# Router casts off VectorE, raw weight pieces ahead in the DMA queue, and new places in a sixteen-step schedule

## The chip, the cores and the metric

One core of a Trainium2 chip. The time is the device time of one execution in microseconds; of the kernel before there are three runs, and their median is the number that counts.

## What is computed

One transformer-like layer on 4 sequences of 1024 tokens with 256 channels, all in float32. First a Mamba block, cut from the reference:

```python
xp, res = jnp.split(x @ W_in.T, 2, axis=-1)
xc = silu(conv1d(xp, conv_w, taps=4) + conv_b)
ssm = xc @ W_x.T                      # 16 of B, 16 of C, 1 of dt
dt = softplus(dt @ W_dt.T + b_dt)
h = exp(A * dt) * h + dt * B * xt     # per token, 512 channels x 16 states
y = einsum(h, C) + D * xt
x = layernorm(x + silu(y + res) @ W_out.T)
```

Then a mixture of 8 experts: a router softmax picks the top 2, each expert is 256 to 1024 (exact gelu) to 256, the two are weighted and added, and a second layernorm follows.

## The kernel before

The 4096 tokens are cut into 8 blocks of 512 (BLOCKS, T), two to a sequence; the states are 16 (STATE). `mamba` (L137) runs the blocks as iterations of sixteen **steps**, one for each state, and each step has four **quarters**, one for each group of 128 channels. In a quarter (n, q) of block i

- TensorE first turns the scaled input of state n into PSUM (`drive`, L458, matmul at L465, into one of two halves of `d_ps`; it waits until the scan two quarters before has read that half), then adds one or two quarters of products of an earlier state into `y_ps` (`sum_states`, L470, L478), then does what a table puts between;
- VectorE runs one scan over 512 tokens (`scan`, L1010, L1021), then what its table puts between;
- ScalarE works two steps ahead (LEAD): `scale` (L747, L756) makes the scaled input and `decays` (L764, L774) the decay, both from rings of three;
- GpSimd multiplies the scan's result with the row of C (`times_c`, L1317, L1327), in two halves a step. For blocks with an even number it also copies the last column away (L1322);
- SP's DMA queue loads the row of C for two steps on (`load_c`, L355) when GpSimd has finished the step before.

Four blocks are in work at a time. While block i is scanned, block i+1 (`front`, f) gets its silu, ssm projection, dt (z spread at L529, sizes at L543, L1056), its inputs dt*x (`inputs`, L1065, L1071) and their turned copies (`turn_u` on TensorE, L551, L557, read by `ut_out` on ScalarE, L868, L873); block i+2 (`early`) its input projection (`in_projection`, L496, L506, read by `xp_out`, L793) and convolution (`tap`, L1025); block i-1 (`back`) its gate, output projection (`out_projection`, L570, L577), residual and first layernorm; block i-2 (`place`) is routed. The gate products (`gate`, L485) and `skip` (L491) go straight into the sum of block i. The place of every such piece is written out by hand as a quarter (tables at L445 to L451 and the `at ==` lines), and each engine does its own in program order, so that a piece that has to wait holds up all behind it. Small results share six PSUM banks of 2 KB a partition (`BANK_OF`, L97); `bank_counts` (L123) derives the semaphore counts from the order of the names.

The router: `logits` (L594) on TensorE, `router_pick` (L1098) on VectorE: copy, top 8 of 8, their indices, three casts (L1117 to L1119) and a comparison with 0..7 that makes a one-hot (L1121); `router_member` (L1390) and `router_shift` on GpSimd; `ranks` (L607, L612, L615), which counts earlier tokens of each expert; `router_rank`, `router_sum`, `router_invert` and `router_place` (L1145) on VectorE, the last with a reduction (L1149) and the cast of the positions to integers (L1151). Then GpSimd sends 8 indirect DMAs of 128 rows each (`send_rows`, L1342, L1349). In the one-hot's place `router_spread` (GpSimd, L1414) puts the positions.

Beside this, the weights of four experts are cut into 64 **pieces** of 128 x 256, of which each is split into a rounded part and its rest: SP loads the raw piece, ScalarE makes the rounded part (`high_part`, L777, L779), GpSimd the rest (`low_part`, L1331, L1334), and SP stores both (`hand_on`, L366) and, right behind it, loads the raw piece that comes next. Eight of them go into each block, at PIECE_STEPS (L296); the ring is two (PARTS_RING).

After block 7, `end` of each engine finishes the last sum, projection and routing, and a table of slots is made. `experts` (L1506) then runs 71 slots of 128 rows, and `combine` (L1839) adds the two outputs and normalises.

## Time and profile before

| | us |
|---|---|
| median of 3 runs | 1548.41 (1547.02 to 1553.11) |
| profiled execution | 1544.33 |
| its span, first to last instruction | 1542.7 |
| TensorE busy (share of the span) | 1340.7 (87%) |
| VectorE | 1153.1 (75%) |
| GpSimd | 1036.7 (67%) |
| ScalarE | 1013.4 (66%) |

In the rows PE is TensorE, DVE VectorE, ACT ScalarE, POOL GpSimd and SP the engine whose queue loads and stores; SPq is that queue. L1021 is line 1021 of the kernel. A row of the timeline gives the start, the length, and in brackets how long the engine sat idle before it and who released it; x4 means four instructions merged into one row. Lengths of instructions that follow one another overlap: the pitch between them is shorter than the mean length. A row of a stretch gives start:end and its length, the busy us (and the count of instructions) of PE, PEld (TensorE's weight loads), DVE, ACT and POOL, then the granted TensorE clock as a share of full speed, the share of time that the DMA engines were busy, and GB/s. A row of a group of instructions ends with its busy us and the mean ns of one, then the idle time before them.

### The profile page before, as it was taken

How to read it: one execution, taken by the hardware profiler on the slowest of the kernel's cores; microseconds unless marked ns; L12 is line 12 of the kernel's file. 1: busy time of each engine (PE TensorE's matmuls, PEld its weight loads, DVE VectorE, ACT ScalarE, POOL GpSimd, SP SyncE). 2: the span in 40 equal slices, each digit the busy share in tenths (PEclk: the TensorE clock that was granted, in tenths of full speed). 3: DMA queues.
4: the chain of work that ended last, by engine and by line, in shares of the span. 5: the costliest groups of instructions: out<-in, count | busy, mean ns of one | idle time of the engine just before them, and what ended most of it. 6: DMA issues, size and time to landing. Idle time of an engine off the chain costs nothing. (4 is left out here: it accounts for less than half of the span.)

```text
span 1542.7 us, 29244 instructions
## 1 busy us (share of the span) xinstructions
PE 1340.7 (87%) x8828; PEld 1119.7 (73%) x8829; DVE 1153.1 (75%) x2010; ACT 1013.4 (66%) x1370; POOL 1036.7 (67%) x981
## 2 busy tenths in 40 slices
PE   4698898998998898998898898199999999999960
PEld 1377677777677677677677687189999999999860
DVE  5678888888988888988877887656666666666546
ACT  4898998979978978978987883234334334433324
POOL 3478787779878878878988998635444444444336
PEclk8699999999999999999999998599999999999985
DMA  7012223222322222322321326421453612311027
GB/s 262 21 56 86 72 65 102 69 87 73 91 86 75 91 84 75 104 70 76 103 73 59 110 76 225 138 74 53 149 167 110 217 41 85 119 38 42 25 70 275
DMA packets 85568, 150.12 MB, mean 97 GB/s; under 512 B 11042, under 2 KB 34210, under 8 KB 85476
## 3 DMA queue, kind: packets, MB, share of 16 engines
q1 hardware_dynamic: 70228, 116.39, 23.6%
q0 software_dynamic: 9888, 27.29, 5.3%
q10 hardware_dynamic: 5360, 5.26, 1.0%
q8 instruction: 52, 0.85, 0.2%
q14 instruction: 40, 0.33, 0.1%
HBM read 104.45 MB, written 44.45 MB: 97 GB/s over the span
## 5 line engine op out<-in xcount | busy, mean ns | idle before, releaser
L1327 POOL TENSOR_TENSOR arena<-arena 128x1024 f32<-128x1024 f32 x256 | 604.1, 2370 | 32.0 <-DVE arena L1021 17.0
L465 PE MATMUL d_ps<-ident,arena 128*128 128x128 f32 x2048 | 331.2, 287 | 59.3 <-DVE arena L1021 56.7
L465 PEld LDWEIGHTS d_ps<-ident,arena 128*128 128x128 f32 x2048 | 248.6, 147 | 177.5 <-issue 89.5
L1021 DVE TENSOR_TENSOR_SCAN arena<-arena,carry,d_ps 128x512 f32<-128x512 f32 x256 | 316.5, 1268 | 49.9 <-PE d_ps L465 47.1
L1021 DVE TENSOR_TENSOR_SCAN arena<-arena,d_ps 128x512 f32<-128x512 f32 x256 | 301.9, 1208 | 63.8 <-PE d_ps L465 61.1
L756 ACT ACTIVATE arena<-u_tok,b_tok 128x512 f32<-128x512 f32 x508 | 324.7, 714 | 5.6 <-PE d_ps L465 4.0
L478 PE MATMUL y_ps<-ident,arena 128*128 128x128 f32 x2048 | 301.8, 278 | 7.3 <-POOL arena L1327 7.3
L1663 ACT ACTIVATE h_t<-ht_ps 128x512 f32<-128x512 f32 x142 | 84.4, 595 | 295.9 <-PE ht_ps L1718 295.9
L774 ACT ACTIVATE arena<-dt,neg_a 128x2048 f32<-128x2048 f32 x128 | 255.5, 1996 | 2.1 <-DVE neg_a L1255 1.1
L478 PEld LDWEIGHTS y_ps<-ident,arena 128*128 128x128 f32 x2048 | 244.0, 144 | 8.5 <-POOL arena L1327 8.2
L1728 PEld LDWEIGHTS y_ps<-arena,h_parts 128*128 128x128 f32 x1704 | 214.6, 193 | 9.0 <-issue 4.2
L1703 PE MATMUL h_ps<-arena,xg_t 128*128 x852 | 216.7, 404 | 3.6 <-DVE xg_t L1798 2.9
L1728 PE MATMUL y_ps<-arena,h_parts 128*128 x1704 | 217.9, 284 | 1.8 <-DVE h_parts L1806 1.8
L1806 DVE TENSOR_TENSOR h_parts<-h_t,h_parts 128x512 fp32r<-128x512 f32 x142 | 98.3, 692 | 118.9 <-ACT h_parts L1665 117.5
L1703 PEld LDWEIGHTS h_ps<-arena,xg_t 128*128 128x128 f32 x852 | 157.5, 192 | 36.0 <-issue 5.7
L1608 POOL TENSOR_TENSOR rest<-b,tags 128x256 f32<-128x256 f32 x71 | 43.2, 609 | 138.0 <-DVE tags L1780 138.0
L1622 POOL DMA_INDIRECT expert_out<-y,dest x71 | 86.7, 1221 | 42.0 <-issue 23.6
L1598 POOL DMA_DIRECT2D xg<-expert_rows x71 | 41.4, 582 | 93.1 <-issue 90.6
L1792 DVE TENSOR_TENSOR h<-h_ps,b 128x512 f32<-128x512 f32 x142 | 91.7, 686 | 9.7 <-PE h_ps L1703 7.9
L1334 POOL TENSOR_TENSOR arena<-arena 128x256 fp32r<-128x256 f32 x64 | 46.8, 731 | 68.9 <-ACT arena L779 68.6
L1665 ACT CAST h_parts<-h_t 128x512 fp32r<-128x512 f32 x142 | 88.1, 620 | 4.5
L1813 DVE SCALAR_TENSOR_TENSOR y<-y_ps,tags,rest 128x256 f32<-128x256 f32 x71 | 34.4, 484 | 55.0 <-PE y_ps L1728 53.3
(220 smaller groups left out, 1712.4 us busy)
## 6 DMA issues: line engine op xcount, KB each, us to landing
arena<-c_rows SPq DMA_DIRECT2D x128, 256.0 KB
arena<-weight_parts SPq DMA_DIRECT2D x20, 1024.0 KB, 5.3
weight_parts<-arena SPq DMA_DIRECT2D x64, 256.0 KB, 3.7
xg<-expert_rows POOLq DMA_DIRECT2D x71, 130.0 KB
arena<-in_pieces SPq DMA_DIRECT2D x16, 512.0 KB, 8.7
arena<-in_pieces SPq DMA_DIRECT2D x64, 128.0 KB, 3.5
arena<-expert_out SPq DMA_DIRECT2D x16, 512.0 KB, 9.8
weight_parts<-arena SPq DMA_DIRECT2D x4, 1024.0 KB, 5.0
```

The source lines that it names most:

```text
L465: last = nc.tensor.matmul(d_ps[:, c % 2, j * P:(j + 1) * P], ub[:, g % U_RING, j, c * P:(c + 1) * P], t.ident[:], start=True, stop=True, i ...
L478: last = nc.tensor.matmul(y_ps[:, j, c * P:(c + 1) * P], h[:, g % H_RING, c, j * P:(j + 1) * P], t.ident[:], start=(n == 0 and c == 0), st ...
L756: nc.scalar.activation(ub[:, g % U_RING, j, :], u_tok[:, j, :], ACT.Identity, scale=b_tok[:, b % 2, j, n:n + 1]).then_inc(scaled, 1)
L774: nc.scalar.activation(decay[:, g % D_RING], dt[:, b % 2], ACT.Exp, scale=t.neg_a[:, n:n + 1])\
L1021: nc.vector.tensor_tensor_scan(h[:, g % H_RING, c, :], decay[:, g % D_RING, c, :], d_ps[:, c % 2, :], 0.0 if i % 2 == 0 else carry[:, n, c ...
L1327: nc.gpsimd.tensor_tensor(h[:, g % H_RING, lo:hi, :], h[:, g % H_RING, lo:hi, :], c_row[:, g % C_RING:g % C_RING + 1, :].broadcast_to([P, ...
L1622: pool.indirect_dma_start(out=d.y, out_offset=bass.IndirectOffsetOnAxis(ap=dest[:, k:k + 1], axis=0), in_=y[:, k, :], in_offset=None).then ...
L1665: nc.scalar.copy(h_parts[:, 0, lo:hi, :], h_t[:, lo:hi, :]).then_inc(h_high, 1)
L1703: last = nc.tensor.matmul(h_ps[:, g, :].rearrange("p (q n) -> p q n", n=PW), xg_t[:, k % 2, xp, c, :], w_r[:, bass.ds(e % W_RING, 1), q:q ...
L1728: last = nc.tensor.matmul(y_ps2[:, k % 2, 0:DIM], h_parts[:, hp, j, :], w_r[:, bass.ds(e % W_RING, 1), PIECES // 2 + j, wp, :].squeeze(1), ...
L1792: nc.vector.tensor_tensor(h[:, g * HALF:(g + 1) * HALF], h_ps[:, g, :], b1[:, bass.ds(e, 1), g * HALF:(g + 1) * HALF].squeeze(1), ALU.add) ...
L1806: nc.vector.tensor_tensor(h_parts[:, 1, lo:hi, :], h_t[:, lo:hi, :], h_parts[:, 0, lo:hi, :].bitcast(F32), ALU.subtract).then_inc(h_low, 1)
```

## The change

- Three casts of `router_pick` become reductions over an axis of length one. The one-hot's comparison reads 0..7 from the logits' PSUM bank, where one more matmul (identity times the row 0..7) puts them; the bank is freed by the comparison, and no longer by the copy of the logits.
- The cast of the positions moves from `router_place` on VectorE to the beginning of `send_rows` on GpSimd.
- On SP's queue the raw piece is loaded two steps after the piece that had its buffer, ahead of that step's store, and no longer behind the store one step after; PIECE_STEPS change.
- Nearly all tables change. TensorE: `turn(1)` from (2,0) to (1,3); logits from (4,1), (4,2), (5,0), (5,2) to (3,0), (3,3), (3,3), (4,0); ranks from (8,0) to (7,3); `turn_y` to (2,1), (2,1), (2,2), (2,2); ssm projection from (2,3), (3,0), (3,2), (3,3) to (2,3), (3,1), (3,1), (3,2); z spread from (4,2) to (5,0); sizes from (8,3), (9,1), (9,1), (9,2) to (8,3), (8,3), (9,3), (10,1); `turn_u` from (13,1), (13,2), (13,3), (14,0) to (13,0), (13,3), (14,0), (14,1); skip from (5,1), (12,3), (13,1), (14,2) to (4,3), (11,3), (11,3), (12,0).
- VectorE: add_sizes to (8,3), (8,3), (9,3), (10,3); inputs from (10,1), (11,1) to (9,3), (11,3); variance from (11,0) to (11,2); `router_rank` from (8,2) to (7,3), `router_sum` from (7,2) to (10,1), `router_place` from (15,2) to (15,1).
- ScalarE: the order within steps changes. `xp_out(2)` goes from step 0 back to step 15; `y_silu` from the end of step 1 to the start of 2; `turned_out` from 2 and 3 to 1 and 2; `ssm_out` from the start of 3 to its end; all four z parts between scale and decays of step 5; `size_exp` and `btok_out` to the end of 5; `router_exp` from 7 to 6; `normed` behind the scale of step 12; `xp_out(0)` and `(1)` to the ends of 11 and 12; `ut_out(0)` from the start of 14 to the end of 13.
- GpSimd: `router_member` and `router_shift` from the end of step 5 into step 6, behind the second product of step 5; `router_spread` from 12 to 7, `router_den` from 9 to 13, `rstds` from the end of 10 to 11, halo sums from 7 to 11; two sends in step 15 instead of one, and the other six at 1, 2, 2, 2, 4, 4 of the next iteration instead of seven at 0, 0, 1, 1, 3, 3, 4.

```diff
-BANK_OF = {"turn0": 0, "turn1": 1, "ssm": 0, "logits": 0, "z": 1, "z2": 2, "btok": 0, "out0": 0, "ranks": 1,
-           "zc0": 1, "zc1": 1, "zc2": 0, "zc3": 1, "out1": 0, "in0": 0, "in1": 1, "ut0": 0, "ut1": 0, "ut2": 0,
+BANK_OF = {"turn0": 0, "turn1": 1, "ssm": 1, "logits": 0, "z": 1, "z2": 2, "btok": 0, "out0": 0, "ranks": 1,
+           "zc0": 1, "zc1": 0, "zc2": 0, "out1": 0, "zc3": 1, "in0": 0, "in1": 1, "ut0": 0, "ut1": 0, "ut2": 0,
...
-        PIECE_STEPS = (1, 3, 5, 7, 9, 11, 13, 15)
+        PIECE_STEPS = (2, 4, 6, 7, 9, 10, 12, 14)
...
                     .then_inc(parts_stored[k % PARTS_RING], 16)
-                nxt = k - 1 + PARTS_RING
-                if k >= 1 and nxt < PARTED:
-                    sp.wait_ge(parts_stored[nxt % PARTS_RING], 16 * (nxt // PARTS_RING))
+
+            def fetch(k):
+                if k < PARTED:
+                    sp.wait_ge(parts_stored[k % PARTS_RING], 16 * (k // PARTS_RING))
                     hold(sp, held_sp)
-                    sp.dma_start(parts[:, nxt % PARTS_RING, 1], raw_piece(nxt))\
-                        .then_inc(raw_loaded[nxt % PARTS_RING], 16)
+                    sp.dma_start(parts[:, k % PARTS_RING, 1], raw_piece(k)).then_inc(raw_loaded[k % PARTS_RING], 16)
...
                         load_c(g + LEAD)
+                    piece = piece_of(*divmod(g - 2, STATE))
+                    if piece is not None:
+                        fetch(piece + PARTS_RING)
                     piece = piece_of(*divmod(g - 1, STATE))
                     if piece is not None:
                         hand_on(piece)
-                    if n == 4 and back:
+                    if n == 5 and back:
...
-                    if n == 7 and early and scans:
+                    if n == 9 and early and scans:
...
-        SUM_AT = [6 + k + max(0, 10 - k // 6) for k in range(4 * STATE)]
-        OUT_AT = (((7, 0), (7, 1), (7, 3), (7, 3), (7, 3), (8, 2), (8, 2), (8, 3)),
-                  ((10, 1), (10, 2), (10, 2), (10, 3), (10, 3), (11, 0), (11, 0), (11, 0)))
-        GATE_AT = ((4, 3), (6, 0), (6, 0), (6, 1), (7, 1), (7, 1), (8, 3), (9, 3))
-        IN_AT = (((11, 1), (11, 2)), ((12, 1), (12, 1)), ((15, 0), (15, 2)), ((15, 3), (15, 3)))
-        TAP_AT = (((11, 3), (12, 0), (12, 1)), ((13, 0), (14, 0), (15, 0)), ((15, 3), (16, 1), (16, 3)),
+        SUM_AT = [5 + k + max(0, 11 - k // 7) for k in range(4 * STATE)]
+        OUT_AT = (((7, 0), (7, 1), (7, 2), (7, 3), (7, 3), (8, 1), (8, 3), (8, 3)),
+                  ((10, 0), (10, 1), (10, 1), (10, 3), (11, 0), (11, 0), (11, 0), (11, 0)))
+        GATE_AT = ((6, 0), (6, 1), (6, 1), (6, 1), (7, 0), (7, 2), (9, 0), (9, 1))
+        IN_AT = (((11, 2), (11, 2)), ((11, 3), (12, 1)), ((15, 0), (15, 0)), ((15, 2), (15, 3)))
+        TAP_AT = (((11, 3), (12, 0), (12, 2)), ((13, 3), (14, 2), (15, 0)), ((16, 0), (16, 1), (16, 2)),
                   ((17, 0), (17, 1), (17, 2)))
...
                     if j == TT - 1:
+                        last = nc.tensor.matmul(bank("logits", p)[:, TT * EXPERTS:(TT + 1) * EXPERTS], t.ident[:],
+                                                t.iota_ef[:], start=True, stop=True)
                         last.then_inc(m_filled[bank_of("logits", p)], 1)
...
                     nc.vector.tensor_copy(logit[:].rearrange("p j e -> p (j e)"),
-                                          bank("logits", p)[:, 0:TT * EXPERTS])\
-                        .then_inc(m_freed[bank_of("logits", p)], 1)
-                    wait_freed(dve, "logits", p)
+                                          bank("logits", p)[:, 0:TT * EXPERTS]).then_inc(picked, 1)
+                    dve.wait_ge(picked, 4 * p + 1)
...
-                    nc.vector.tensor_copy(rows_of(p)[:, :, DIM + 1], idx[:, :, 0])
-                    nc.vector.tensor_copy(rows_of(p)[:, :, DIM + 3], t.token2[:, p, :])
-                    nc.vector.tensor_copy(ek[:], idx[:, :, 0:TOPK]).then_inc(picked, 1)
                     dve.wait_ge(picked, 4 * p + 3)
+                    nc.vector.tensor_reduce(rows_of(p)[:, :, DIM + 1], idx[:, :, 0:1], AXX, ALU.add)
+                    nc.vector.tensor_reduce(rows_of(p)[:, :, DIM + 3], t.token2[:, p, :].unsqueeze(2), AXX, ALU.add)
+                    nc.vector.tensor_reduce(ek[:], idx[:, :, 0:TOPK].unsqueeze(3), AXX, ALU.add).then_inc(picked, 1)
+                    dve.wait_ge(picked, 4 * p + 4)
                     nc.vector.tensor_tensor(
                         onehot[:].rearrange("p j k e -> p (j k) e"),
-                        t.iota_ef[:].unsqueeze(1).broadcast_to([P, TT * TOPK, EXPERTS]),
+                        bank("logits", p)[:, TT * EXPERTS:(TT + 1) * EXPERTS].unsqueeze(1)
+                        .broadcast_to([P, TT * TOPK, EXPERTS]),
                         ek[:].rearrange("p j k -> p (j k)").unsqueeze(2).broadcast_to([P, TT * TOPK, EXPERTS]),
-                        ALU.is_equal).then_inc(picked, 1)
+                        ALU.is_equal).then_inc(m_freed[bank_of("logits", p)], 1)
...
                 def router_place(p=p):
                     dve.wait_ge(spread, p + 1)
-                    if p == BLOCKS - 1:
-                        dve.wait_ge(rows_sent[p % 2], 16 * TT * TOPK * (p // 2))
+                    dve.wait_ge(place_chain, p)
                     nc.vector.tensor_reduce(rk[:], onehot[:], AXX, ALU.add).then_inc(pos_done, 1)
-                    dve.wait_ge(pos_done, 2 * p + 1)
-                    nc.vector.tensor_copy(pos[:, p % 2], rk[:]).then_inc(pos_done, 1)
-                    dve.wait_ge(pos_done, 2 * p + 2)
...
             def send_rows(b, m):
                 if m == 0:
-                    pool.wait_ge(pos_done, 2 * b + 2)
+                    pool.wait_ge(pos_done, b + 1)
+                    if b == BLOCKS - 1:
+                        pool.wait_ge(rows_sent[b % 2], 16 * TT * TOPK * (b // 2))
+                    nc.gpsimd.tensor_copy(pos[:, b % 2], rk[:]).then_inc(place_chain, 1)
+                    pool.wait_ge(place_chain, b + 1)
...
                 def router_member(p=p):
-                    pool.wait_ge(picked, 4 * p + 4)
+                    wait_freed(pool, "logits", p)
```

## Rows read from the trace of the kernel before

**Rows 1.** Blocks 2 and 7 as stretches: length, busy us of PE, PEld, DVE, ACT, POOL, clock, DMA.
```profile
...
273.60:385.60 112.00, 103.39 (x698) 82.91 (x697) 96.14 (x115) 98.34 (x122) 89.29 (x84) 0.97 0.24 76
...
841.30:943.20 101.90, 89.16 (x678) 78.31 (x678) 90.07 (x99) 75.04 (x93) 94.37 (x64) 0.98 0.28 87
```

**Rows 2.** The same columns, block 4 cut into groups of steps.
```profile
...
524.55:536.74 12.19, 12.19 (x101) 10.88 (x100) 9.46 (x8) 12.19 (x17) 9.86 (x10) 1.00 0.13 47
536.74:545.38 8.64, 7.43 (x48) 5.25 (x47) 8.28 (x23) 8.52 (x12) 7.39 (x6) 1.00 0.55 184
545.38:568.99 23.61, 23.61 (x146) 17.61 (x145) 18.44 (x24) 20.71 (x22) 22.65 (x25) 1.00 0.14 41
568.99:585.56 16.57, 14.92 (x105) 12.64 (x104) 14.96 (x19) 10.84 (x16) 10.05 (x12) 1.00 0.42 128
...
591.49:602.11 10.62, 7.58 (x54) 7.34 (x53) 5.42 (x5) 6.81 (x10) 10.30 (x11) 0.84 0.31 86
...
sum 114.18, PE 103.39 PEld 82.55 DVE 95.68 ACT 97.74 POOL 97.05; mean PE 12.92 PEld 10.32 DVE 11.96 ACT 12.22 POOL 12.13
```

**Rows 3.** Timeline of block 4, steps 6 and 7 (start, length, engine, line).
```profile
...
542.02 5.66 DVE L1021 TENSOR_TENSOR_SCAN arena<-arena,d_ps 128x512 f32<-128x512 f32 x5
...
546.22 0.25 POOL L1392 TENSOR_TENSOR member<-onehot 128x32 f32<-128x32 f32 x1
...
546.88 2.37 POOL L1327 TENSOR_TENSOR arena<-arena 128x1024 f32<-128x1024 f32 x1
...
```

**Rows 4.** Waits, 275 to 840 us (who <- for whom: total, times, longest).
```profile
DVE arena L1021 <- PE d_ps L465: 69.9, 79, 4.6
...
ACT arena L779 <- DMA arena<-in_pieces: 44.8, 15, 9.1
...
```

**Rows 5.** Timeline of block 2, steps 7 and 8, TensorE.
```profile
...
319.12 1.88 PE L486 MATMUL y_ps<-w_in,x_t 128*128 128x512 f32 x4
...
323.02 1.46 PE L577 MATMUL m_ps<-w_out,tmp 128*128 128x256 f32 x6
...
325.33 1.04 PE L615 MATMUL m_ps<-member,ones 128*128 128x32 f32 x8
...
```

**Rows 6.** Groups of VectorE's instructions, 275 to 840 us (busy us, mean ns).
```profile
...
L1117 DVE CAST xrow<-idx 128x4 f32<-128x4 uint32 x5 | 5.4, 1081 | 0.2
L1121 DVE TENSOR_TENSOR onehot<-iota_ef,ek 128x64 f32<-128x64 f32 x5 | 5.4, 1079 | 0.2
L1151 DVE CAST pos<-rk 128x8 uint32<-128x8 f32 x5 | 4.5, 908 | 0.2
...
L1149 DVE TENSOR_REDUCE rk<-onehot 128x8 f32<-128x64 f32 x5 | 1.0, 193 | 0.0
...
```

**Rows 7.** Timeline of block 7's end.
```profile
...
937.39 4.47 DVE L1151 CAST pos<-rk 128x8 uint32<-128x8 f32 x1
...
942.72 1.09 POOL L1349 DMA_INDIRECT expert_rows<-xrow,pos  x1 [0.89 <-DVE pos L1151]
...
```

**Rows 8.** Timeline of block 3, step 13.
```profile
...
476.68 0.36 SPq L375 DMA_DIRECT2D arena<-in_pieces  x1
...
478.68 1.99 ACT L774 ACTIVATE arena<-dt,neg_a 128x2048 f32<-128x2048 f32 x1
...
482.06 0.41 ACT L779 CAST arena<-arena 128x256 fp32r<-128x256 f32 x1 [1.39 <-DMA arena<-in_pieces]
...
483.00 1.11 PE L557 MATMUL m_ps<-ident,y_u 128*128 128x128 f32 x4 [3.43 <-ACT u_tok L873]
...
485.01 1.28 DVE L1021 TENSOR_TENSOR_SCAN arena<-arena,carry,d_ps 128x512 f32<-128x512 f32 x1 [4.55 <-PE d_ps L465]
```

**Rows 9.** DMA issues on the page (count, KB each, us to landing).
```profile
...
weight_parts<-arena SPq DMA_DIRECT2D x64, 256.0 KB, 3.7
...
```

**Rows 10.** Timeline of block 4, VectorE's inputs.
```profile
...
571.24 1.20 DVE L1071 TENSOR_TENSOR y_u<-dt,xc 128x1024 f32<-128x1024 f32 x1
...
579.87 2.30 DVE L1071 TENSOR_TENSOR y_u<-dt,xc 128x1024 f32<-128x1024 f32 x1
...
```

More of the change, by code:

```diff
@@ L953, in step @@
                     if place and n == 2:
-                        turned_out(0)
-                    if front and n == 3:
-                        ssm_out()
-                    if place and n == 3:
                         turned_out(1)
-                    if front and n == 5:
-                        z_part(2)
-                    if front and n == 6:
-                        btok_out()
-                    if place and n == 7:
-                        router_exp()
-                    if early and n == 12:
-                        xp_out(e, 0)
-                    if back and n == 12:
-                        normed()
-                    if early and n == 13:
-                        xp_out(e, 1)
                     if front and n == 14:
-                        ut_out(0)
                         ut_out(1)
@@ L977, in step @@
                         scale(g + LEAD)
-                    if front and n == 4:
+                    if place and n == 1:
+                        turned_out(0)
+                    if front and n == 5:
                         z_part(0)
                         z_part(1)
-                    if front and n == 6:
+                        z_part(2)
                         z_part(3)
+                    if back and n == 12:
+                        normed()
+                    if early and n == 15:
+                        xp_out(e, 2)
                     if 0 <= g + LEAD < STEPS:
@@ L986, in step @@
                         high_part(piece_of(i, n))
-                    if back and n == 1:
-                        y_silu()
                     if back and n == 2:
                         yt_copy()
-                    if front and n == 6:
+                    if front and n == 3:
+                        ssm_out()
+                    if front and n == 5:
+                        btok_out()
                         size_exp()
+                    if place and n == 6:
+                        router_exp()
                     if front and n == 7:
                         size_log()
+                    if early and n == 11:
+                        xp_out(e, 0)
+                    if early and n == 12:
+                        xp_out(e, 1)
+                    if front and n == 13:
+                        ut_out(0)
             iterations(act, step)
@@ L1433, in end @@
                     router_shift()
-                    for m in range(1, 4):
+                    for m in range(2, 4):
                         send_rows(BLOCKS - 3, m)
@@ L1481, in step @@
                         router_weigh()
-                    if place and n == 5:
-                        router_member()
-                        router_shift()
-                    if back and n == 10:
-                        rstds()
                     if place:
-                        for m, when in enumerate((15,)):
+                        for m, when in enumerate((15, 15)):
                             if n == when:
```

66 lines of the change are left out of this document (35 added, 31 removed).

## The prediction

> **What bounds the kernel now.** I read the busy time by stretches first. The span has a scan part (eight blocks of sixteen steps, 55 to 943 us), a short joint to about 1004 us, and the expert and combine parts, which the change doesn't touch. Block 2 begins at 273.6 and block 7 at 841.3 [rows 1], so a middle block takes 567.7 / 5 = 113.5 us; everything below is a sum over such blocks. In block 4 TensorE is busy 103.4 of 114.2 us, ScalarE 97.7, GpSimd 97.1 and VectorE 95.7 [rows 2]: no engine is full, and what sets the pace differs from step to step. The same rows, by steps, show it. In steps 4 to 5 and in steps 7 to 9 TensorE is busy for all of 12.19 and 23.61 us while VectorE has gaps; these are TensorE's. In step 6 VectorE is the fuller (8.28 of 8.64). In step 13 nobody is but GpSimd: 10.62 us for VectorE work of 5.42. VectorE's scans follow at 5.66 / 5 = 1.13 us [rows 3], so four of them alone are 4.5 to 4.7 us, the floor of a step.
>
> The waits of the five blocks say the same: the scan waits 69.9 us for its d_ps input from TensorE (79 times), which is 14 us a block; ScalarE waits 44.8 us for raw weight pieces [rows 4].
>
> **The change, part by part.** A tally of each step, as the larger of two sums: TensorE's (four drives and about four and a half state sums, at 4 x 0.11 us each by the pitch of L615, 3.5 to 4.0 us, plus what stands between) and VectorE's (4.6 plus its extras). From [rows 5]: a gate product is 2 of the 4 matmuls that take 1.88 us at 0.43 each, so 0.86; an output product 2 of six in 1.46, so 0.43; the ranks' ten about 1.1; logits of one tile 4 x 0.11 = 0.44; a skip 8 x 0.11 = 0.87. The other 512-wide products (ssm, sizes, input halves) are taken like a gate. For steps 7 to 9 of before this gives 7.8 + 8.1 + 7.4 = 23.3 against 23.61 measured, so I trust it to about 0.3 a step.
>
> 1. Casts off VectorE. The three casts of the pick and the cast of the positions work on 4 to 8 elements, yet the means are 1081 ns (L1117) and 908 ns (L1151), against 193 ns for the reduction L1149 beside them, which handles 64; the comparison L1121 also has 1079 [rows 6]. One L1151 took 4.47 us [rows 7]. The long ones end as GpSimd's product ends. They become reductions (0.16 to 0.19), the comparison reads its constants from PSUM, and the position cast moves to GpSimd. Over the five blocks the excess is 5 x (0.92 + 0.92 + 0.74) = 13 us of VectorE, 2.6 a block. Not all is on the path: a delayed pick lets TensorE finish its gates. By the tally step 6 after it is TensorE's: 4.0 + four gates 3.4 + 0.2 = 7.6, against 8.64. I take -1.0 for step 6, and nothing in 15, where TensorE's 3.96 + 3.44 = 7.4 covers it. GpSimd's cast of 8 elements has no row; between its member addition, 0.25 [rows 3], and a send, 1.09 [rows 7], I take 0.25 (nearest in size), beside other work. The matmul that puts the constants into PSUM is one of 0.11, twice that at most.
>
> 2. DMA queue. Before, SP issues a store and, behind it, the next raw piece, for use one step on. In block 3 it was issued at 476.68; ScalarE, free at 480.67, got it at 482.06, and only then made the copy that TensorE waited for: 3.43 us of TensorE, 4.55 of VectorE [rows 8]. After, the raw piece goes ahead of the store of its step and, where the spacing is 2, two steps early. No step of the queue is removed: per step one c row, at most one fetch, one store. The new wait, for the store of one step earlier, holds back the x loads behind it; a store of 256 KB lands in 3.7 us [rows 9] and a step is 7, so zero. I count 1.4 us a block here, inside step 13.
>
> 3. turn_u and ut_out. ut_out(0) moves from step 14 to the end of 13, and turn_u spreads from three quarters of 13 to (13,0), (13,3), (14,0), (14,1). The copy is then ready about when (13,3) asks, and the later ones one quarter apart. Step 13: tally 5.4, plus 1 to 2 of wait left, so 7.0 against 10.62: -3.6. This is the largest term, with bounds -1 (the wait only moves to step 14) and -5.2 (none left).
>
> 4. Steps 4 to 5: gate and two logits leave; what stays is one logit, a skip and the z spread: 5.0 + 5.1 = 10.1 against 12.19: -2.1. It needs ScalarE two microseconds earlier there; ssm_out, turned_out and two z parts move behind decays(6), which gives 2.1 us back, so it just fits. Bounds 0 and -2.6.
>
> 5. Steps 7 to 9: ranks moves into step 7 (4.0 + five outputs 2.15 + two gates 1.7 + ranks 1.1 = 8.9), which relieves 8 and 9 (7.3, 6.8): 23.0, -0.6.
>
> 6. Other steps: three taps instead of two in step 0 (+0.7), ssm and logits together in 3 (+0.3), step 2 -0.3; 10 to 11 6.6 + 10.2 against 16.57, +0.2; 12, 14, 15 even. Together +0.9. More work lands in one quarter (two skips at (11,3)); I put +0.5 a block on that.
>
> 7. A price that VectorE keeps: inputs (L1071) reads two SBUF tiles. In block 4 its first half took 1.20 us, the second 2.30 [rows 10]. The first half runs where GpSimd stands idle for ScalarE's piece; if item 2 ends that idleness, it can take the longer form. Between 0 and +1.1 a block, I take +0.8. The Trainium skill (page "SBUF — State Buffer", section "Who interferes with whom") states that a VectorE instruction with two SBUF inputs contends with a GpSimd one that reads SBUF; it speaks against the change here, and the two durations fit it. By it alone the term would be the +1.1, and the sum 2 us worse.
>
> Sum for block 4: -1.0 - 3.6 - 2.1 - 0.6 + 0.9 + 0.5 + 0.8 = -5.1, and -5.0 for the mean block. Five blocks -25. Block 1 has no router and no casts, but items 3 and 4: -3 (estimate). Block 0 has neither router nor output projection, and its turn_u wait has other neighbours: -2 (estimate). Block 7 has TensorE light and GpSimd at 94.4 of 101.9 [rows 1]: the long cast of 4.47 goes, but the first send of that block now stands on GpSimd with a second (1.1 us) and the position copy ahead of the last product: -1 and +0.5. Total -30.5. The profiled execution took 1544.33 us, so 1513.8; the median of the three runs is 4.1 higher, at 1548.41, and the forecast is given on its scale: **1518 us**.
>
> **The rivals.**
> *TensorE stays the bound.* Its stretches at 100% [rows 2] are only reshuffled; cast time was hidden and step 13's wait moves to 14. Then item 3 gives -1, item 4 -0.7, item 1 -0.5, and +1 of clumping: about -1.2 a block, -8 in all: 1540. For it: TensorE's work is the same plus one matmul. Against: it idles 10.8 us a block, most of it in 13 and 11.
> *More than forecast.* Every block comes down to TensorE's 103.4 busy: 5 x -10 and -4 at the ends: 1494.
> *Slower: the ranks wait.* router_member moved behind the second product of step 5 in GpSimd's order. In block 4 the member ran at 546.22 and that product from 546.88 to 549.25 [rows 3], 12.5 us after step 6 began (536.74). ranks is now wanted at (7,3), by the tally 7.6 + 6 = 13.6 after it. GpSimd's low part of the piece at step 2 now waits for ScalarE's silus, and three sends (1.1 each) follow it, so it may be later than today. Each microsecond past 1.1 is paid by TensorE, and by VectorE's rank behind it, in six blocks. At 5 us past, all of the gain is gone; at 7, with ScalarE's item 4 not fitting, the time is 1548 + 10 = 1558. For it: GpSimd lags VectorE most just there. Against: its shorter steps before and the c rows' distance leave it a microsecond.
> *It doesn't do what it says.* The reductions, or the PSUM comparison, are held by GpSimd like the casts: 13 us of VectorE and 4.3 in block 7 come back, a third on the path: 1525 to 1530. L1149 at 193 ns, always beside a long cast's place, speaks against [rows 6].
>
> **How the numbers follow.** Forecast (1506 to 1531) 0.60; TensorE stays the bound (1531 to 1548) 0.18, half of it within 0.5%; more than forecast 0.07; doesn't do what it says 0.04; ranks wait 0.11, of it 0.08 slower and 0.03 the same. A measurement tells about 0.5%, 7.7 us, from no change. Faster 0.60 + 0.09 + 0.07 + 0.04 = 0.80; same 0.12; slower 0.08. The range reaches down to items 3, 4 and 7 at their good bounds, 5 x -3 more, 1502, and up into the TensorE case: 1541. Left out: about 0.05 below, 0.14 above.
>
> **What would show it.** L1117, L1119 and L1121 near 0.2 us in every block; step 13 at 7 us, no wait of TensorE's L557 over 2 us; the piece wait of ScalarE under half of 44.8; steps 4 to 5 near 10; a middle block near 108.5. Wrong if a middle block keeps over 112; if VectorE's rank or TensorE's ranks matmuls wait over 2 us; if the first half of inputs stays at 1.20 my item 7 is wrong, in the good direction.

## The result, and the profile after

| | median us (runs) | ratio to before, 95% |
|---|---|---|
| before, beside it | 1549.59 (1547.02 to 1553.11) | |
| after | **1496.41** (1495.88 to 1496.80) | 0.9655 (0.9634 to 0.9676) |

The kernel is 53 us faster. The forecast was 1518 with a range down to 1502: the direction was right, the size too small by 22 us, and the time lies below the range. The page of the profiled execution (1495.88 us), its span and busy times:

```profile
span 1494.2 us, 29280 instructions
...
PE 1320.8 (88%) x8844; PEld 1100.9 (74%) x8845; DVE 1122.4 (75%) x2002; ACT 1011.9 (68%) x1370; POOL 1042.4 (70%) x989
```

Against the table of before, TensorE's and VectorE's busy time fell, by 20 and 31 us, though TensorE got one matmul more a block. The span fell by 48.5 us. By the starts of the blocks' first scans that is 1.5 before block 0, 5.1 in block 0, 4.1 in block 1, 35.3 in the five middle blocks (567.7 to 532.4) and 2.4 from block 7's start to the end. The other 4 to 5 us between 48.5 and 53 are scale: the profiled execution of before was the quickest of its runs.

Blocks 2 to 6 as stretches, with the columns of [rows 1], one block and the sum of the five:

```profile
262.80:368.80 106.00, 101.00 (x700) 79.93 (x699) 91.72 (x114) 98.11 (x122) 89.95 (x85) 1.00 0.27 81
...
sum 532.40, PE 503.50 PEld 400.22 DVE 465.58 ACT 488.44 POOL 471.88; mean PE 100.70 PEld 80.04 DVE 93.12 ACT 97.69 POOL 94.38
```

The sum of the same five blocks in the kernel before:

```profile
sum 567.70, PE 516.84 PEld 414.31 DVE 482.02 ACT 490.11 POOL 472.49; mean PE 103.37 PEld 82.86 DVE 96.40 ACT 98.02 POOL 94.50
```

VectorE runs the scans, so its time divides the gain: 482.0 - 465.6 = 16.4 us less work and 85.7 - 66.8 = 18.9 us less standing still. ScalarE and GpSimd work as much as before.

Block 4 by steps, cut as in [rows 2] (in order: steps 0 to 3, 4 to 5, 6, 7 to 9, 10 to 11, 12, 13, 14 to 15):

```profile
476.88:502.25 25.37, 21.97 (x146) 16.93 (x145) 22.48 (x22) 25.31 (x28) 22.23 (x20) 0.93 0.23 79
502.25:513.15 10.90, 10.67 (x88) 9.40 (x87) 9.24 (x8) 10.90 (x16) 10.43 (x9) 1.00 0.27 87
513.15:522.29 9.14, 7.74 (x46) 5.25 (x45) 6.19 (x23) 9.02 (x12) 8.49 (x9) 1.00 0.32 98
522.29:545.87 23.58, 23.58 (x153) 18.29 (x152) 18.94 (x22) 22.24 (x27) 22.96 (x21) 1.00 0.39 115
545.87:561.60 15.73, 15.73 (x105) 12.70 (x104) 13.39 (x21) 10.96 (x16) 12.34 (x14) 1.00 0.34 110
561.60:568.00 6.40, 6.30 (x52) 5.57 (x51) 5.88 (x6) 6.25 (x11) 6.24 (x5) 1.00 0.09 34
568.00:573.09 5.09, 5.07 (x45) 4.58 (x44) 5.09 (x7) 3.48 (x4) 4.93 (x6) 1.00 0.17 46
573.09:584.27 11.18, 11.18 (x80) 8.93 (x79) 10.60 (x14) 10.07 (x15) 10.55 (x15) 1.00 0.27 79
sum 107.39, PE 102.24 PEld 81.64 DVE 91.80 ACT 98.24 POOL 98.17; mean PE 12.78 PEld 10.21 DVE 11.47 ACT 12.28 POOL 12.27
```

Step 13 went from 10.62 to 5.09 and is now full of VectorE work. Step 6 did not get shorter (8.64 to 9.14), though VectorE's work in it fell from 8.28 to 6.19: something else sets it now. Waits of the five middle blocks, 262.8 to 795.2 us, columns as in [rows 4]:

```profile
DVE arena L1024 <- PE d_ps L468: 60.9, 86, 2.6
...
PE m_ps L528 <- DVE onehot L1123: 6.8, 5, 1.4
```

The scan's wait for TensorE fell from 69.9 to 60.9 us (the rows of before have the same values for its own five blocks), in more and shorter pieces: 86 with a longest of 2.6, where there were 79 with a longest of 4.6. ScalarE's 44.8 us for raw pieces are gone. New is TensorE's wait for the comparison, which now frees the PSUM bank. The groups that answer to [rows 6], 275 to 800 us (L1119 was the cast L1117, L1123 is the comparison):

```profile
L1119 DVE TENSOR_REDUCE xrow<-idx 128x4 f32<-128x4 uint32 x5 | 0.8, 161 | 0.2
...
L1123 DVE TENSOR_TENSOR onehot<-m_ps,ek 128x64 f32<-128x64 f32 x5 | 1.1, 224 | 0.2
```

The cast (1081 ns) became 161 ns and the comparison (1079) 224 ns. The position cast, now on GpSimd, is short there but for one of eight, at 922 us, when the blocks' scans are over (minimum, median, maximum in ns):

```profile
L1346 POOL CAST pos<-rk x8: 187/198/1208, 370.9 to 937.6; 128x8 uint32<-128x8 f32 x8
```

### The profile page after: what moved, and what is told of

Its sections match the earlier page's. It is cut to its first block and busy times, and to the rows that moved or that the text cites. A ratio compares the mean times of both kernels' runs of the same rounds, so it can differ in the third digit from the quotient of the medians.

```text
span 1494.2 us, 29280 instructions
## 1 busy us (share of the span) xinstructions
PE 1320.8 (88%) x8844; PEld 1100.9 (74%) x8845; DVE 1122.4 (75%) x2002; ACT 1011.9 (68%) x1370; POOL 1042.4 (70%) x989
## 5 line engine op out<-in xcount | busy, mean ns | idle before, releaser
L468 PEld LDWEIGHTS d_ps<-ident,arena 128*128 128x128 f32 x2048 | 240.5, 144 | 149.6 <-issue 70.8
L468 PE MATMUL d_ps<-ident,arena 128*128 128x128 f32 x2048 | 323.0, 282 | 30.8 <-DVE arena L1024 26.0
L1024 DVE TENSOR_TENSOR_SCAN arena<-arena,carry,d_ps 128x512 f32<-128x512 f32 x256 | 313.5, 1264 | 45.0 <-PE d_ps L468 44.8
L481 PE MATMUL y_ps<-ident,arena 128*128 128x128 f32 x2048 | 298.0, 274 | 12.3 <-POOL arena L1326 12.3
L481 PEld LDWEIGHTS y_ps<-ident,arena 128*128 128x128 f32 x2048 | 239.3, 142 | 14.1 <-POOL arena L1326 14.1
L1721 PE MATMUL ht_ps<-ident,h 128*128 128x128 f32 x568 | 73.8, 273 | 0.5 <-DVE h L1795 0.5
```

The costliest lines, as they stand in the source:

```text
L468: last = nc.tensor.matmul(d_ps[:, c % 2, j * P:(j + 1) * P], ub[:, g % U_RING, j, c * P:(c + 1) * P], t.ident[:], start=True, stop=True, i ...
L481: last = nc.tensor.matmul(y_ps[:, j, c * P:(c + 1) * P], h[:, g % H_RING, c, j * P:(j + 1) * P], t.ident[:], start=(n == 0 and c == 0), st ...
L1024: nc.vector.tensor_tensor_scan(h[:, g % H_RING, c, :], decay[:, g % D_RING, c, :], d_ps[:, c % 2, :], 0.0 if i % 2 == 0 else carry[:, n, c ...
```

## The experiments

Each time is the median of its runs. The ratio is to runs of the kernel before that stood beside them, in four sets with medians of 1551.7, 1549.15, 1549.21 and 1548.99 us. In the expectations A is the theory of the prediction; the other letters are rivals, each said where it first stands.

### One part alone, on the kernel before

`b_casts`: only the reductions, the PSUM constants and the position cast on GpSimd. `b_turnu`: only

```diff
-for j, when in enumerate(((13, 1), (13, 2), (13, 3), (14, 0))):
+for j, when in enumerate(((13, 0), (13, 3), (14, 0), (14, 1))):
```

with `ut_out(0)` at the end of ScalarE's step 13. `b_dma`: only the order on SP's queue, `hand_on` without its load and `fetch(piece + PARTS_RING)` ahead of it, with the old PIECE_STEPS. `b_all3`: the three together.

> The kernel before with the cast part alone (reductions, constants from PSUM, position cast on GpSimd). Theory A (the gain of 53 us is a sum of parts, none of them over half): the casts are worth some 8 to 12 us here, because step 6 falls from 8.4 only to about 7.6 (TensorE's products, and turn_b now waits for the comparison to free bank 0) and step 15 in two blocks by 1.1, block 7 gains its 4.5 us: 1538 to 1541. Theory B (the casts and what they hold up are most of the gain): 1520 or less. Theory C (step 13's wait is most of it): within 4 us of before, 1545 to 1549.

> The kernel before with the new places of turn_u and of ut_out(0) alone. Theory A: step 13 falls from 9.95 on average to about 7 (the late raw piece no longer stands ahead of ut_out(0), since with the old places of the pieces there is one at step 13, so it does stand there still): -12 to -18 us, 1531 to 1537. Theory B: -5 or less. Theory C: -25 or more.

> The kernel before with the new order of the DMA queue alone. ScalarE's wait for raw pieces should fall from 9 us a block to under 3. Theory A: only the part inside step 13 reaches the end, 1.4 to 2 us in the blocks where it stood (3, 4, 5), and some 0 to 1 elsewhere: -5 to -9 us, 1540 to 1544. Theory B: nothing, 1547 to 1549. Theory C (step 13's wait is most of the gain, and the DMA most of that wait): -15 or more.

> The three parts together on the kernel before, all other tables old. Theory A: their sum and a little more, since step 13 is freed only by two of them together (5.3 a block instead of 9.95): 1515 to 1522, and the other tables are worth the 20 to 25 us that remain. Theory B and C: 1505 or less, the other tables only reshuffle.

| | us | ratio, 95% | to before |
|---|---|---|---|
| b_casts | 1539.75 | 0.9926 (0.9907 to 0.9945) | -12 |
| b_turnu | 1541.82 | 0.9942 (0.9921 to 0.9963) | -10 |
| b_dma | 1512.43 | 0.9750 (0.9731 to 0.9769) | **-39** |
| b_all3 | 1507.45 | 0.9710 (0.9678 to 0.9742) | -44 |

`b_casts` came as expected, `b_turnu` gave less, `b_dma` far more, and `b_all3` lies between its two expectations. The queue's order alone is nearly three quarters of the whole gain; the prediction had given it 1.4 us a block. The parts add up to 61 and give 44 together, for two of them cure the same wait: step 13, 9.95 us on the mean of the five middle blocks, falls to 6.52 in `b_dma`, to 7.44 in `b_turnu`, and only to 5.40 in `b_all3` (steps are measured here from first scan to first scan). The other tables and the new PIECE_STEPS bring the rest, 0.9710 to 0.9655: some 8 us. PIECE_STEPS were not tried by themselves. `b_dma` in its five middle blocks, and its steps 10 to 11 and 13 of block 4:

```profile
552.91:567.79 14.88, 14.33 (x101) 12.05 (x100) 14.20 (x19) 10.38 (x16) 10.92 (x12) 1.00 0.43 134
...
573.72:580.39 6.67, 5.94 (x54) 5.67 (x53) 5.43 (x5) 5.18 (x8) 6.51 (x6) 1.00 0.31 90
...
sum 544.00, PE 507.18 PEld 403.79 DVE 479.67 ACT 491.37 POOL 471.97; mean PE 101.44 PEld 80.76 DVE 95.93 ACT 98.27 POOL 94.39
```

Step 13 falls from 10.62 to 6.67 without `turn_u` being touched. Of 567.7 - 544.0 = 23.7 us, VectorE's work is 2.4 and its standing still 21.3. By steps, on the mean of the five blocks, it is 3.4 us in step 13 and 1.5 in step 11, and little elsewhere. So the queue took away the waits, and what `after` has on top (11.6 us in these blocks) goes with less work: 14.1 us of VectorE's. The casts and the comparison are 15 us shorter, and the inputs are 2.4 longer again.

### What held the queue

The waits of the SP queue itself, 54 to 945 us, in the kernel before (the first row is the c rows' normal pace):

```profile
SPq L42 <- POOL arena L1327: 674.8, 113, 29.3
SPq L42 <- PE y_ps L486: 92.1, 6, 17.7
```

After:

```profile
SPq L42 <- PE y_ps L489: 2.8, 4, 1.4
```

SP waited six times, 92.1 / 6 = 15.4 us on the mean, for the gate products. That is the wait ahead of the x load (`sp.wait_ge(gates_done, i + 1)` at step 7), whose last gate stood at (9,3). The timeline of block 4, steps 7 to 10, of the kernel before shows what stood behind it:

```profile
554.50 0.32 SPq L363 DMA_DIRECT2D arena<-c_rows  x1
...
568.61 0.33 SPq L428 DMA_DIRECT2D x_t<-in_x_t  x1
...
569.52 0.37 SPq L369 DMA_DIRECT2D weight_parts<-arena  x1
570.00 0.37 SPq L375 DMA_DIRECT2D arena<-in_pieces  x1
...
574.72 0.41 ACT L779 CAST arena<-arena 128x256 fp32r<-128x256 f32 x1 [7.01 <-DMA arena<-in_pieces]
575.20 0.72 POOL L1334 TENSOR_TENSOR arena<-arena 128x256 fp32r<-128x256 f32 x1 [6.04 <-ACT arena L779]
```

For 14 us SP issues nothing. Then the x load, a c row, the store and only at 570.00 the raw piece of step 9 go out; ScalarE stands 7.01 us and GpSimd 6.04. ScalarE is late from here on, and when it comes to step 13 another piece holds it, as in [rows 8]. The new `fetch` loads the piece ahead of this wait; the whole change also moves the wait two steps on and the last gate to (9,1). `b_xload` and `b_swap` take these apart, on the kernel before:

```diff
-                    if n == 7 and early and scans:        # b_xload
+                    if n == 9 and early and scans:
```
```diff
+                nxt = k - 1 + PARTS_RING                  # b_swap: the load ahead of the store, same step
+                if k >= 1 and nxt < PARTED:
+                    ...
                 sp.wait_ge(low_done, k + 1)
```

> The kernel before with one digit changed: SP's load of the next x block stands at step 9 instead of step 7. There it waits for the last gate product (9,3), 15 to 18 us in each of six blocks (92.1 us in all), and the c row, the store and the next raw piece stand behind it. Theory D (the held queue is where the 38 us of the queue's order come from: ScalarE then waits 7 us for the piece of step 9, comes late to ut_out(0), and TensorE and VectorE wait in step 13): most of it comes back by this digit alone, -15 to -32 us, 1518 to 1535. Theory E (it is the place of the raw piece behind the store in the ring, at every step): -5 or less.

> The kernel before with the raw piece issued ahead of the wait for low_done and of the store, within the same step, for use one piece on; nothing else. Theory E (place behind the store): most of the 38 us, -20 to -35, 1516 to 1531. Theory D (the wait of step 7 ahead of it, or the lead): -3 to -10, since the piece of step 9 is still issued only when the gates are done.

`b_xload` took 1524.91 us, 0.9845 (0.9797 to 0.9892): **one digit gives -24**. `b_swap` took 1531.74, 0.9887 (0.9846 to 0.9929): -17. Both together (`b_xswap`), and the x load moved on top of the full queue order (`b_xdma`):

> The kernel before with both small edits: x load at step 9, and the raw piece ahead of the store within the step (one step of lead). Theory H (lateness of the raw piece at ScalarE is the whole cause, however it comes about): the wait for raw pieces falls under 10 us and the time to that of the queue's new order, 1510 to 1516. Rival (the two-step lead has a worth of its own): 1518 to 1524.

> The kernel before with the queue's new order and the x load at step 9. Theory H: the lead covered the held queue already, so nothing is added to the 1512.4 of the order alone: 1509 to 1514. Rival (the held queue costs something beside the raw pieces, by c rows that come late to GpSimd, 6 us of waits in the profile of the order alone): 1502 to 1508.

`b_swap` came between its two expectations. `b_xswap` took 1521.11, 0.9817 (0.9792 to 0.9841), -28, where the rival had its range: the two mend mostly the same thing, and both together are still some 10 us short of `b_dma`, whose raw piece is also fetched two steps ahead. Some 5 us of that are in step 13, with 7.59 us on the mean of the five blocks against 6.52. `b_xdma` took 1516.7, 0.9787 (0.9767 to 0.9807), -32: no gain on top of `b_dma`, and 4 us more in the medians, though the two intervals just touch. In the profiled executions it is 4.6 us, and 3.6 of them are steps 6 and 7 of one block, in which two of the pick's instructions were held and not one:

```profile
413.77 1.79 DVE L1120 CAST xrow<-idx 128x4 f32<-128x4 uint32 x1
...
415.73 2.35 DVE L1124 TENSOR_TENSOR onehot<-iota_ef,ek 128x64 f32<-128x64 f32 x1
```

ScalarE's wait for raw pieces, 54 to 945 us, goes with the times but for that last case. Of the 67.5 us of before, 42 stand ahead of the pieces of step 9, those behind the x load. Before, `b_xload`, `b_xswap`, `b_dma`, one fence each:

```profile
ACT arena L779 <- DMA arena<-in_pieces: 67.5, 25, 9.1
```
```profile
ACT arena L779 <- DMA arena<-in_pieces: 26.4, 21, 4.9
```
```profile
ACT arena L779 <- DMA arena<-in_pieces: 17.2, 16, 3.1
```
```profile
ACT arena L782 <- DMA arena<-in_pieces: 4.5, 1, 4.5
```

67.5, 26.4, 17.2, 4.5 us of waiting stand beside 1549, 1525, 1521, 1512 us (`b_swap` has 55.5 and 1532, with step 9's 40 still in it; `b_xdma` 4.1 and 1517). In `b_dma` the queue itself waits for the gates as long as ever:

```profile
SPq L42 <- PE y_ps L489: 92.7, 6, 17.3
SPq L42 <- DMA weight_parts<-arena: 23.2, 6, 4.0
```

So the long wait in the queue costs nothing by itself. What cost was the load that stood behind it and was needed soon. The second row is the new wait for the store, 23.2 us in six times. `b_xdma` has neither this wait nor most of the first (28.7 us left), and it is no faster.

### One part undone, from the kernel after

`a_dma`, `a_turnu` and `a_casts` are the reverse of the three parts above, but for one thing: `a_dma` has the old order with the new PIECE_STEPS. `a_x7` puts the x load back to step 7.

> The changed kernel with the old order of the DMA queue (raw piece behind the store, for use one piece on), new places of the pieces. Theory A: ScalarE waits again for raw pieces, up to 3 us each, but its lead of 8 to 14 us in steps 9 to 15 hides most; +2 to +8, 1498 to 1504. Theory C: step 13's wait comes back, +15 or more.

> The changed kernel with turn_u and ut_out(0) at their old places. There is no raw piece at step 13 any more, so TensorE waits for ScalarE's decay only, about 2.2 us as in block 1 of before. Theory A: +2.2 to 3 in seven blocks, +15 to +21: 1511 to 1517. Theory B: under +5. Theory C: +25 or more.

> The changed kernel (1496.4) with the casts put back on VectorE as before, all tables new. Theory A: +10 to +15 us (VectorE is nearer to the bound now, and each cast that meets a GpSimd product costs up to 2.4 us; the wait of turn_b for bank 0 goes, -1.5 a block): 1503 to 1511. Theory B: +30 or more. Theory C: +0 to +3.

> The changed kernel with the x load back at step 7. Its last gate is at (9,1), so SP is held 10 to 12 us a block again. Theory H (the lead covers it): +0 to +5, 1496 to 1501. Rival: +10 or more.

| | us | ratio to before, 95% | to after |
|---|---|---|---|
| a_dma | 1524.43 | 0.9840 (0.9799 to 0.9881) | **+28** |
| a_turnu | 1502.42 | 0.9707 (0.9668 to 0.9747) | +6 |
| a_casts | 1511.08 | 0.9764 (0.9725 to 0.9804) | +15 |
| a_x7 | 1496.36 | 0.9660 (0.9644 to 0.9677) | 0 |

`a_turnu` cost less than theory A had, `a_dma` far more; `a_casts` and `a_x7` came as expected. From this side the queue's order is again the largest term, but not by the same wait. In `a_dma` the x load stands at step 9, no wait of SP's for the gates is left, and still ScalarE waits 82 us for raw pieces. Of these, 35 are at the pieces of step 7 and 32 at those of step 10, in every block: each is the second of two pieces that PIECE_STEPS now puts one step apart, and by the old order it is loaded only behind the store in its own step. So this +28 is the price of the old order with the new places, and doesn't confirm the price of the held queue, which rests on `b_xload`. With only the x load back at step 7 SP waits 65 us for the gates and ScalarE 23.0 us for raw pieces, and the time stays; that ScalarE has the lead to bear it is the likely reason, not tested. `a_dma`, then `a_x7`:

```profile
ACT arena L781 <- DMA arena<-in_pieces: 82.0, 23, 5.8
```
```profile
ACT arena L784 <- DMA arena<-in_pieces: 23.0, 8, 5.4
```

Either place of the x load will do once the piece is fetched first. The single runs of `a_casts` differ as no other kernel's do: 1492.54 in the profiled one, 1510.67 to 1512.66 in the others. Its profile therefore shows an execution in which the casts cost nothing, and no row of it is used here; the +15 is that of the others. `a_sbuf`, next, was also quickest in its profiled execution, so its rows show less than its median.

### The comparison's operands

`a_sbuf`: the kernel after, with the comparison reading 0..7 from SBUF again.

```diff
-                        bank("logits", p)[:, TT * EXPERTS:(TT + 1) * EXPERTS].unsqueeze(1)
-                        .broadcast_to([P, TT * TOPK, EXPERTS]),
+                        t.iota_ef[:].unsqueeze(1).broadcast_to([P, TT * TOPK, EXPERTS]),
```

With it the copy of the logits frees the bank again, and the matmul of the constants is gone.

> The changed kernel with the comparison reading 0..7 from SBUF and the copy freeing the logits' bank, as before; the three reductions stay. TensorE's turn_b no longer waits 1.6 us a block for the bank (five of five blocks). Theory A (that new wait is on the path): TensorE reaches drive (6,2) earlier, -1.5 a block where the comparison isn't caught, but the comparison with two SBUF inputs is held by GpSimd up to 2.2 us in some blocks: -4 to +4, 1492 to 1500. Rival (the bank wait is hidden under the pick anyway): 0 to +8, by the held comparison alone.

It took 1518.24 us (1509.0 in the profiled run, up to 1522.1), 0.9816 (0.9774 to 0.9857): +22 for one instruction a block, where little was expected. The row of that instruction, eight blocks, in ns:

```profile
L1122 DVE TENSOR_TENSOR onehot<-iota_ef,ek x8: 225/1012/6991, 301.4 to 936.2; 128x64 f32<-128x64 f32 x8
```

The same comparison takes 224 ns from PSUM and up to 6991 from SBUF. It was 1079 ns on the mean in the kernel before, beside a cast of 1081. One by one, in blocks 3 and 4 of that kernel, it is the one or the other:

```profile
424.37 1.78 DVE L1117 CAST xrow<-idx 128x4 f32<-128x4 uint32 x1
...
426.32 0.22 DVE L1121 TENSOR_TENSOR onehot<-iota_ef,ek 128x64 f32<-128x64 f32 x1
...
539.36 0.17 DVE L1117 CAST xrow<-idx 128x4 f32<-128x4 uint32 x1
...
539.71 2.39 DVE L1121 TENSOR_TENSOR onehot<-iota_ef,ek 128x64 f32<-128x64 f32 x1
```

Of the seven picks up to 947 us, five have a long cast (1.47 to 2.75 us) and a short comparison, the other two a short cast and a long comparison (2.39 and 2.33). The long one ends within 0.1 us of the end of one of GpSimd's products. Mostly the first of the pick's instructions that meets a product is held and what follows gets through, but not always: in one block a second cast took 0.71 us, and in `b_xdma` a cast and the comparison were both held. So the casts had to go *and* the comparison had to leave SBUF. With the casts alone gone only the comparison is left to meet the product, and it can pay more: 1.63, 6.99, 0.23, 6.97 and 0.23 us in blocks 2 to 6 of `a_sbuf`. The 6.99 runs beside three products of GpSimd that follow one another without a gap (407.64 to 414.63), so it did not get in between them. Step 6 takes 14.1 us in those two blocks and 7.8 in the other three. `a_sbuf`'s 1518 us are no better than `a_casts` with both undone (1511). The Trainium skill (page "SBUF — State Buffer", section "Who interferes with whom") states that a VectorE operation with two SBUF inputs contends with a GpSimd one that reads SBUF, that a copy or cast in a 2-port mode does too, that whoever issues first has the shared pair of ports for the whole instruction, and that on trn2 a reduction never contends. This case agrees: 161 ns for the reduction against 1081 for the cast, 224 against up to 6991 for the comparison. That these casts ran in such a mode no row shows.

### What sets step 6 now

The timeline of block 3, step 6, of the kernel after:

```profile
407.37 0.22 DVE L1123 TENSOR_TENSOR onehot<-m_ps,ek 128x64 f32<-128x64 f32 x1
...
407.65 0.42 PE L528 MATMUL m_ps<-ident,ssm 16*128 16x16 f32 x4 [1.43 <-DVE onehot L1123]
...
408.00 2.84 PE L489 MATMUL y_ps<-w_in,x_t 128*128 128x512 f32 x6
...
410.68 0.60 PE L468 MATMUL d_ps<-ident,arena 128*128 128x128 f32 x4
...
411.32 2.45 DVE L1024 TENSOR_TENSOR_SCAN arena<-arena,carry,d_ps 128x512 f32<-128x512 f32 x2 [2.53 <-PE d_ps L468]
```

TensorE waits 1.43 us with a small turn (L528, `btok` in BANK_OF) for the bank that the comparison frees, runs three gates (six matmuls) at (6,1), and the scan then waits 2.53 for its input. Two causes are possible, the bank and the gates. `a_btok` takes the wait for the comparison away, by another bank for that turn; `a_btokg` also moves one gate a quarter on; `a_btokg2` spreads them where VectorE's pick covers them.

```diff
+EARLY_BANK = {"btok": 3, ...}                             # a_btok, with "btok": 1 in BANK_OF
-GATE_AT = ((6, 0), (6, 1), (6, 1), (6, 1), (7, 0), (7, 2), (9, 0), (9, 1))
+GATE_AT = ((6, 0), (6, 1), (6, 1), (6, 2), (7, 0), (7, 2), (9, 0), (9, 1))   # a_btokg
+GATE_AT = ((5, 3), (6, 0), (6, 1), (6, 1), (6, 2), (7, 2), (9, 0), (9, 1))   # a_btokg2
```

> The changed kernel with turn_b's output in bank 1 (bank 3 for block 0) instead of bank 0, which the comparison frees late. In the profile after, TensorE waits 1.6 us for it in each routed block, and the scan (6,2) 2.6 us. Theory F (that wait is on the path): step 6 falls from 9.2 to about 7.8, -6 to -9 us over six blocks: 1487 to 1491. Rival G (the three gates behind it set the step anyway): 0 to -3.

> As a_btok, and one gate moved from (6,1) to (6,2), behind the drive that the scan waits for. Theory F: a little better than a_btok, -1 more. Rival G: this is the part that counts, -4 to -6 against 1496.

> As a_btokg (1492.1), with the five gates of steps 6 and 7 one or two quarters earlier: (5,3), (6,0), (6,1), (6,1), (6,2) instead of (6,0), (6,1), (6,1), (6,2), (7,0). If the scan's waits in steps 6 and 7 are TensorE's gates in quarters where VectorE has nothing beside the scan, (7,1) loses its 1.1 us and (6,0) gets 0.5: -2 to -4, 1488 to 1490. Rival (the sum over steps 5 to 8 is TensorE's whatever the places): within 1 us.

`a_btok` 1496.13, 0.9664 (0.9623 to 0.9704): the wait for the comparison is gone and the time stays. That doesn't clear the bank, for the other bank is late too. Block 4:

```profile
516.18 0.42 PE L528 MATMUL m_ps<-ident,ssm 16*128 16x16 f32 x4 [0.59 <-ACTq L855]
```

TensorE now waits for ScalarE, which reads z out of that bank, and step 6 of this block falls from 9.14 to 8.41 us (from 9.21 to 8.65 on the mean of five). `a_sbuf` shows what is left: the copy frees the bank early, the turn of this block waits for nobody, the three gates stand at (6,1) as in `after`, and step 6 takes 7.8 us in the three blocks whose comparison took 1.63 us or less. So the late bank is on the path, at some 1.3 us a block, of which `a_btok` gets back 0.6.

`a_btokg` 1492.08, 0.9642 (0.9601 to 0.9684), -4 in the median, within its interval of nothing. `a_btokg2` **1489.80**, 0.9616 (0.9600 to 0.9632), all four runs between 1489.56 and 1490.40: below every run of the kernel after, and the lowest median of all versions. The largest part of its gain over `a_btok` is in step 7, 8.69 to 7.79 us on the mean of the five blocks, for the gate at (7,0) is gone from there; step 6 moved by 0.2. Places and bank both count, then, and a bank that is free in time together with the new places was not tried. The scan's wait for TensorE, 54 to 945 us, falls from 102.0 us in `after`, first below, to 89.8 in `a_btokg2`, second, in more pieces:

```profile
DVE arena L1024 <- PE d_ps L468: 102.0, 132, 4.9
```
```profile
DVE arena L1024 <- PE d_ps L468: 89.8, 142, 4.9
```

## Why the prediction was too small

**The step that failed** is item 2: "I count 1.4 us a block here, inside step 13". Alone it measured 23.7 / 5 = 4.7 us in a middle block and 39 us in all. The item read the queue at the one place where TensorE was seen waiting for a late piece, and counted that piece's own 1.39 us. It followed ScalarE's wait of 44.8 us [rows 4] no further, and never asked what SP was waiting for. The place, step 13, was right: the five middle blocks gave 4.7 us a block there against the 3.6 of item 3. The cause and the reach were not. The queue's order alone gives 3.4 us in step 13 and 1.5 in step 11, where the forecast had +0.2 for steps 10 to 11. The view for it, the waits of the SP queue, holds the answer in one row: 92.1 us for L486. "No step of the queue is removed" was true and misleading, for a wait of 15 us stood in the middle of it, ahead of a load that was due: with that wait moved and nothing else, `b_xload` gave 24 us. The diff had even moved that wait (step 7 to 9, and the last gate from (9,3) to (9,1)), and the forecast passed over both as moves.

Point by point:

- **Item 1, casts**: -1.0 in step 6 held for the casts alone: block 4's step 6 is 8.64 before and 7.62 in `b_casts`. In the whole change it rose by 0.5, since three gates now stand together at (6,1) and the turn ahead of them waits for the comparison to free the bank, a wait that the item left out. "Nothing in 15" was low: step 15 fell by 0.6 us on the mean in `b_casts`. In size the item was low. VectorE's work fell by 14.1 us over five blocks beyond `b_dma`, the pick's and the position's 15 less the inputs' 2.4, near the 13 forecast as excess; but the forecast put only 5 of it on the path, and undoing the item costs 15 us, doing it alone gives 12. The durations came as forecast (161 and 224 ns).
- **The new wait, "so zero"**: it is not zero in the queue (23.2 us in `b_dma`), but nothing shows that it costs anything, as said.
- **Item 3, turn_u**: "This is the largest term" was wrong. Step 13 did fall, by 5.5, past the bound of 5.2, but `b_dma` has 3.95 of it. The new places alone are worth 10 us from before and 6 from after, about one a block. The bounds had been set from what TensorE's wait could shrink to, with the wrong cause behind it.
- **Item 4, steps 4 to 5**: -1.3 against -2.1. **Item 5**: 0.0 against -0.6. **Item 6**: steps 0 to 3 of block 4 rose by 1.4 where +0.7 was taken; steps 10 to 11 fell by 0.8 where +0.2 was taken, and with the queue's order alone they fell by 1.7.
- **Steps 14 to 15**, taken as even, gave 1.4. The forecast had let TensorE's products cover step 15. That part of them runs over into the next block's steps 0 to 3, which rose by as much, is likely and not shown.
- **Item 7, inputs**: nearly nothing against the kernel before, and not as forecast. The first half takes 3.14 us in two of five blocks and 1.22 to 1.42 in the others, and the second half, which took up to 2.90 before, takes 1.20 in all five. Block 3 of the kernel after:

```profile
436.07 3.14 DVE L1074 TENSOR_TENSOR y_u<-dt,xc 128x1024 f32<-128x1024 f32 x1
...
451.35 1.20 DVE L1074 TENSOR_TENSOR y_u<-dt,xc 128x1024 f32<-128x1024 f32 x1
```

The ten of the five middle blocks take 15.8 us before, 16.1 after and 13.7 in `b_dma`. So the queue's order by itself made them shorter, and the new places took 2.4 us back, 0.5 a block.

- **Blocks 0, 1 and 7**: -5.1, -4.1, and -2.4 from block 7 on, against -2, -3 and -0.5. The queue's wait is in blocks 0 and 1 as well; `b_dma` gives 2.7 and 4.0 there.
- **The scale**: 4.1 us were added for the median over the profiled execution. After, the two agree within 0.6 us, so the whole addition was missed.

In us of the trace: forecast -30.5, measured -48.5, of which 10 in the middle blocks, 3.1 and 1.1 in blocks 0 and 1, 1.9 from block 7 on and 1.5 ahead of block 0.

Of the rivals, **more than forecast** (1494, given 0.07) is where it came out, though not by its mechanism: the middle block is at 106.5 and not at 103.4, and TensorE's own busy time fell to 100.7. The **ranks wait** did not come: VectorE's rank waits 1.0 us for TensorE's ranks over five blocks, and TensorE's ranks do not stand among the waits. **TensorE stays the bound** was wrong in its time and right in part: the scan's wait for it fell only from 69.9 to 60.9 us, and nearly half of it now lies in steps 6 to 8.

**Left open**: why the last 10 us between `b_xswap` and `b_dma` need two steps of lead, beyond their place in step 13; what the new PIECE_STEPS are worth by themselves; and why `a_casts` varies from run to run. Raw pieces can be fetched further ahead only with a ring of three, which was not tried.

## What to carry to other kernels

When an engine waits for a DMA, look at the issuing queue's own waits before pricing the transfer: a load that is due may stand behind a semaphore wait for something that is needed much later, and then its place in the queue can be worth more than its bytes. Put the load that is due first, and the one with slack, with its wait, behind it. And when small VectorE operations show durations far over their size, change together all neighbours that GpSimd can hold: mending one can hand the wait to the next. When an experiment removes a wait, look whether another has taken its place before calling the first one harmless.

## What the runs showed of the hardware

- A comparison of 64 elements a partition with both inputs in SBUF took 225 to 6991 ns; with one of them in PSUM, a mean of 224 ns.
- In seven picks of the kernel before either the cast of 4 elements was long, at up to 2.75 us, or the comparison behind it; in one block of `b_xdma` both were (1.79 and 2.35 us). A long one ended within 0.1 us of a GpSimd product's end, and one of 6.99 us lasted over three such products.
- Casts written as reductions over an axis of one take 150 to 161 ns for 4 to 8 elements, and a GpSimd cast of 8 elements has a median of 198.
- The granted clock was 0.84 in step 13 of block 4, where TensorE was busy for 7.58 of 10.62 us [rows 2], and 1.00 in the same step after, busy for 5.07 of 5.09. Over the middle blocks it rose from 0.95 to 0.97, to 0.98 to 1.00, and TensorE's busy time there fell by 2.6% (516.8 to 503.5 us) with as many matmuls and one more a block.
